# Weights of the last network quantised by VectorE in 36 steps of 512 columns, one in each of 36 rounds of the causal attention

## The reference, cut to what matters

```python
    def lpbq_dequant(w):
        O, I = w.shape
        qmax = 2.0 ** (W_BITS - 1) - 1.0
        wb = w.reshape(O, I // BLOCK, BLOCK)
        s = jnp.maximum(jnp.max(jnp.abs(wb), axis=-1, keepdims=True) / qmax, 1e-12)
        wq = jnp.clip(jnp.round(wb / s), -qmax - 1.0, qmax) * s
        return wq.reshape(O, I)
```

## Time and profile before

| | us |
|---|---|
| median of 3 runs | 1998.86 |
| lowest, highest | 1998.55, 1998.88 |
| profiled execution, its own time | 1991.99 |
| its span | 1990.2 |
| mean granted clock of TensorE, share of full | 0.932 |
| busy: PE, VectorE, ScalarE, GpSimd | 1727.6, 1380.0, 1019.0, 463.2 |

### The profile page before, as it was taken

The page is one execution under the profiler, slowest core; times in us unless marked ns, Lnnn a source line. Parts: engine busy times, 40 slices in busy tenths (PEclk is TensorE's granted clock), DMA queues, the critical chain, the costliest instruction groups (busy, mean ns, idle before and its releaser), DMA issues.

```text
span 1990.2 us, 34704 instructions
## 1 busy us (share of the span) xinstructions
PE 1727.6 (87%) x12889; PEld 1256.4 (63%) x12889; DVE 1380.0 (69%) x4830; ACT 1019.0 (51%) x2647; POOL 463.2 (23%) x501
## 2 busy tenths in 40 slices
PE   3688888888869888999999999999779999979808
PEld 1456666667653455766767766766669989864307
DVE  6877888888335885777776577777566666753785
ACT  5555655555438543555554355555244555533752
POOL 4000000000000223333333234334323333220003
PEclk7798888998979979999999999999889999999859
DMA  5100000000000201000000000000324243300001
GB/s 163 43 1 1 1 1 1 1 1 2 1 1 0 43 21 70 1 1 1 1 2 1 1 1 2 1 1 2 98 64 96 66 96 78 83 1 0 0 0 43
DMA packets 86078, 49.56 MB, mean 25 GB/s; under 512 B 40223, under 2 KB 83669, under 8 KB 85717
## 3 DMA queue, kind: packets, MB, share of 16 engines
q1 hardware_dynamic: 80195, 47.18, 9.1%
q10 hardware_dynamic: 5714, 0.16, 0.2%
HBM read 45.24 MB, written 2.10 MB: 24 GB/s over the span
## 4 chain that ended last, share of the span: by engine, by line
PE 58%; DVE 26%; ACT 9%; issue 4%; POOL 3%; DMA 0%; POOLq 0%; ACTq 0%; DVEq 0%
PE PS L2079 6%; PE PS L1747 6%; DVE nx L774 5%; DVE sq L783 5%; PE PS L1759 5%; PE PS L1772 4%; PE PS L2513 3%; ACT px L1817 3%; PE PS L1733 3%; PE PS L2143 3%; PE PS L1709 3%; PE PS L1787 2%; PE PS L1720 2%; PE PS L2099 2%; PE PS L828 2%
## 5 line engine op out<-in xcount | busy, mean ns | idle before, releaser
L1817 ACT ACTIVATE px<-PS,cnm 128x896 f32<-128x896 f32 (+7 forms) x256 | 189.2, 756 | 285.6 <-DVE cnm L1882 285.6
L1924 POOL TENSOR_SCALAR px<-px,crl 128x640 f32<-128x640 f32 (+7 forms) x128 | 232.3, 1824 | 371.5 <-DVE crl L1893 371.5
L783 DVE TENSOR_SCALAR sq<-nx 128x4 f32<-128x4 f32 x1024 | 175.5, 171 | 31.4
L774 DVE TENSOR_TENSOR_SCAN nx<-sq 128x6 f32<-128x6 f32 x1024 | 174.0, 170 | 32.0 <-POOL sq L913 0.9
L1880 DVE TENSOR_REDUCE cm<-PS 128x1 f32<-128x512 f32 (+3 forms) x224 | 153.9, 687 | 44.6 <-PE PS L1747 44.6
L1759 PE MATMUL PS<-ident,px 128*128 128x128 f32 x1152 | 156.3, 281 | 9.3 <-ACT pT L1830 6.4
L2183 ACT ACTIVATE YT<-YT,xnm 128x154 f32<-128x154 f32 x256 | 104.8, 413 | 92.8 <-DVE xnm L2214 92.8
L198 POOL TENSOR_SCALAR rstd<-mv 128x1 f32<-128x1 f32 x80 | 34.0, 425 | 506.6 <-DVE mv L176 506.5
L1747 PE MATMUL PS<-kT,qT 64*128 64x512 f32 (+3 forms) x768 | 147.9, 503 | 0.4
L1759 PEld LDWEIGHTS PS<-ident,px 128*128 128x128 f32 x1152 | 124.3, 141 | 36.6 <-ACT pT L1830 23.9
L1772 PEld LDWEIGHTS PS<-pT,V 128*64 128x64 f32 x2304 | 124.7, 137 | 34.4 <-issue 32.5
(11 more groups left out here) (336 smaller groups left out, 3855.0 us busy)
## 6 DMA issues: line engine op xcount, KB each, us to landing
xbs<-in_fside_Bx16xSxS SPq DMA_DIRECT2D x8, 1232.0 KB, 6.6
fsrc<-in_fside_Bx16xSxS SPq DMA_DIRECT2D x8, 1232.0 KB, 6.7
xmk<-in_mask_Bx16xSxS_bk SPq DMA_DIRECT2D x8, 308.0 KB, 8.3
fsrc<-in_mask_Bx16xSxS_bk SPq DMA_DIRECT2D x8, 308.0 KB, 8.3
X<-in_x SPq DMA_DIRECT2D x4, 512.0 KB, 6.8
w<-in_L_attn_W_ffn SPq DMA_DIRECT2D x2, 1024.0 KB, 13.0
t<-in_L_ffn_w SPq DMA_DIRECT2D x2, 1024.0 KB, 11.0
out<-xs SPq DMA_DIRECT2D x16, 128.0 KB, 1.7
```

What stands on the lines that cost most here:

```text
L774: e.tensor_tensor_scan(k.nx[:, t % 2, :], d0, d1, 0.0, ALU.mult, ALU.add).then_inc(sem("rec.scan"), 1)
L783: e.tensor_scalar(place(c % 2 * 2 * W6 + 6 * n + 7), state, 10.0, -10.0, ALU.min, ALU.max).then_inc(sem("rec.clip"), 1)
L1817: e.activation(k.px[n % 2][:, h, c0:c1], row[:, c0:c1], ACT.Exp, scale=-1.0, bias=k.cnm[:, h, slot:slot + 1], accum_out=k.cl[:, h, slot:sl ...
L1924: e.tensor_scalar(x, x, k.crl[:, 0, slot:slot + 1], None, ALU.mult).then_inc(sem("c.normal0"), 1)
```

## The change

The twelve `f.weight` steps leave `extra` in `tail_order`. Each matrix is cut into three parts of 512 columns, and each part keeps its four steps: 36 steps `("f.weight", n, part, i)`. Each is appended to `beside` of one round, so it stands at the end of that round for VectorE: after the projections' copies, before the maxima of the next round. The rounds are 10 to 35 (26 steps, in order) and 45 to 54 (10 steps). The maxima and scales of a part fit in 16 columns, `k.fam` and `k.fs`, which are now reused from part to part. The pieces that PE turns wait for the count 21, 42 or 63 of one semaphore, seven operations for each part. The tail keeps 11 `flip` steps and one more, 12 in ten rounds.

```diff
+    weights = [("f.weight", n, part, i) for n in range(3) for part in range(3) for i in range(4)]
+    for n, step in zip([*range(10, ahead - 1), *range(ahead + 8, len(rounds))], weights):
+        beside[n].append(step)
...
     for n, nm in enumerate(k.fraw):
-        extra += [[("f.weight", n, i)] for i in range(4)]
         n0 = len(k.flips)
...
-    def weight(n, i):
-        v = list(k.fraw.values())[n].rearrange("p (b q) -> p b q", q=32)
-        over = lambda t: bass.AP(t, n * bl, [[3 * bl, P], [1, bl], [0, 32]])
+    def weight(n, part, i):
+
+        v = list(k.fraw.values())[n][:, part * 512:(part + 1) * 512].rearrange("p (b q) -> p b q", q=32)
+        over = lambda t: bass.AP(t, 0, [[16, P], [1, 16], [0, 32]])
+        first = 7 * (3 * n + part)
         if i == 0:
             w.wait_ge("load.swiglu", 48)
...
+            w.wait_ge("fw", first)
+            e.tensor_reduce(k.fam[:, :], v, AX.X, ALU.max, apply_absolute_value=True).then_inc(sem("fw"), 1)
+            w.wait_ge("fw", first + 1)
+            e.tensor_scalar(k.fs[:, :], k.fam[:, :], 1.0 / 7.0, 1e-12, ALU.mult, ALU.max).then_inc(sem("fw"), 1)
+            w.wait_ge("fw", first + 2)
+            e.reciprocal(k.fam[:, :], k.fs[:, :]).then_inc(sem("fw"), 1)
         elif i == 1:
...
             e.tensor_tensor(v, v, over(k.fam), ALU.mult).then_inc(sem("fw"), 1)
         elif i == 2:
...
             e.tensor_scalar(v, v, MAGIC, MAGIC, ALU.add, ALU.subtract).then_inc(sem("fw"), 1)
...
             e.tensor_scalar(v, v, 7.0, -8.0, ALU.min, ALU.max).then_inc(sem("fw"), 1)
         else:
-            w.wait_ge("fw", 6 * n + 6)
-            e.tensor_tensor(v, v, over(k.fs), ALU.mult).then_inc(sem("fw.done"), 1)
+            w.wait_ge("fw", first + 6)
+            e.tensor_tensor(v, v, over(k.fs), ALU.mult).then_inc(sem("fw"), 1)
```

More of the change, by code:

```diff
@@ L330, in flip @@
         if kind in ("gate", "up", "down"):
-            w.wait_ge("fw.done", 1 + ("gate", "up", "down").index(kind))
+            w.wait_ge("fw", 21 * (1 + ("gate", "up", "down").index(kind)))
         if ("flip", n) in k.room:
@@ L1530, in causal_tiles @@
     k.crl = sb("crl", [P, 2, 4], scope=inner)
+    k.fam = sb("fam", [P, 16], scope=inner)
+    k.fs = sb("fs", [P, 16], scope=inner)
     k.wqkv = [sb(f"w{n}T", [P, DC, H * 64], scope=inner) for n in "qkv"]
@@ L1952, in cross_tiles @@
 def cross_tiles(k, sb, sc):
-    k.fam = sb("fam", [P, 3, IC * D // 32], scope=sc)
-    k.fs = sb("fs", [P, 3, IC * D // 32], scope=sc)
     k.x1w = {n: sb("x1" + n, [P, DC, H * 64], scope=sc) for n in "qg"}
@@ L2388, in swiglu_vector @@
     sem, at, PS = k.sem, k.order.at, k.PS
-    bl = IC * D // 32
     s = lambda n: k.stp[:, n:n + 1]
-    def weight(n, i):
-        v = list(k.fraw.values())[n].rearrange("p (b q) -> p b q", q=32)
-        over = lambda t: bass.AP(t, n * bl, [[3 * bl, P], [1, bl], [0, 32]])
+    def weight(n, part, i):
+        v = list(k.fraw.values())[n][:, part * 512:(part + 1) * 512].rearrange("p (b q) -> p b q", q=32)
+        over = lambda t: bass.AP(t, 0, [[16, P], [1, 16], [0, 32]])
+        first = 7 * (3 * n + part)
         if i == 0:
             w.wait_ge("load.swiglu", 48)
[L2397 to L2401, removed]
+            w.wait_ge("fw", first)
[4 more added lines that the diff above has]
+            e.reciprocal(k.fam[:, :], k.fs[:, :]).then_inc(sem("fw"), 1)
         elif i == 1:
-            w.wait_ge("fw", 6 * n + 3)
+            w.wait_ge("fw", first + 3)
             e.tensor_tensor(v, v, over(k.fam), ALU.mult).then_inc(sem("fw"), 1)
         elif i == 2:
-            w.wait_ge("fw", 6 * n + 4)
+            w.wait_ge("fw", first + 4)
             e.tensor_scalar(v, v, MAGIC, MAGIC, ALU.add, ALU.subtract).then_inc(sem("fw"), 1)
-            w.wait_ge("fw", 6 * n + 5)
+            w.wait_ge("fw", first + 5)
             e.tensor_scalar(v, v, 7.0, -8.0, ALU.min, ALU.max).then_inc(sem("fw"), 1)
         else:
-            w.wait_ge("fw", 6 * n + 6)
-            e.tensor_tensor(v, v, over(k.fs), ALU.mult).then_inc(sem("fw.done"), 1)
+            w.wait_ge("fw", first + 6)
+            e.tensor_tensor(v, v, over(k.fs), ALU.mult).then_inc(sem("fw"), 1)
     def tile(T):
```

## The result

| | before | after |
|---|---|---|
| median of 4 runs, us | 1998.7 | 1986.36 |
| lowest, highest | 1997.61, 1998.88 | 1985.86, 1988.23 |
| profiled execution, its own time | 1991.99 | 1985.86 |
| its span | 1990.2 | 1984.0 |

After to before is 0.9938, with an interval from 0.9923 to 0.9953. The change gains 12.3 us by the medians, where I had forecast 5.0, and the time lies 0.14 us under my range.

What follows compares the result with a forecast made beforehand. PE was taken to bound the causal attention, VectorE and GpSimd to set the old tail's end. The tail's -17.0 and the causal attention's +12 sum to -5.0 us: 1998.86 becomes 1993.9 us, range 1986.5 to 1999.0.

Steps and rivals of the forecast that it cites:

- What bounds each stage: PE bounds the causal attention, VectorE and GpSimd the old tail; a round's end has 6.6 us of room in nine rounds.
- The tail, -17.0: Tail: without the twelve weight steps its stalls go and PE bounds it, a gain of 17.0 us.
- The walk's end: Tail: PE's work added step by step, the cross attention's first projection starting at 1442.6 to 1443.0 instead of 1459.96.
- The causal rounds, +12: Causal attention: 36 added steps make PE late by 9.3 us, then 2.5 more, 11.8 in all, taken as 12.
- The wait for GpSimd: Causal attention: steps behind VectorE's scaling wait for GpSimd, 0.4 to 0.7 us in four rounds of nine, 1.7 a block.
- The slack of PE, 0.75: Causal attention: late exponentials delay PE only beyond a slack, 0.75 us in five rounds of nine and more elsewhere.
- The price of a step: Causal attention: maximum with scaling and reciprocal 1.20 us, product 0.72, two roundings 0.92; mean 0.89, 8.0 in nine rounds.
- Rival B: Causal attention: steps mostly hide, without GpSimd's wait or with longer PE slack; cost 5.7, net -11.3, 1987.6 us; chance 0.20.
- Rival C: Causal attention: no slack for PE, or dearer steps; cost 15 to 16, net -1.5, 1997.4 us; chance 0.20.
- D: Causal attention: PE stalls in most rounds and its granted clock falls, so the kernel is slower, 2004 us; chance 0.07.
- The edit does not touch what separates them: Whole kernel: the median's 6.9 us above the profiled run was taken to stay, so the forecast starts from 1998.86.
- my own sign for checking: Start of the cross attention: its first projection was to come 5 us earlier if the forecast was right.

Runs made afterwards that it cites:

- early place: The changed kernel with its 36 steps ahead of 1/sum of head 0 instead of at the round's end; rounds 10 to 70 took 539.61 us, ratio 0.9914.
- maxima only: The changed kernel with its products and roundings replaced by maxima over as many columns, weights unquantised; rounds 10 to 70 took 545.54 us, ratio 0.9933.
- five rounds tested: The changed kernel without its 36 steps, one 512-column maximum ending rounds 14, 23, 32, 50 and 59; rounds 10 to 70 took 542.58 us.
- middle place: The changed kernel with each step between VectorE's copy of a turned piece and 1/sum of head 1; rounds 10 to 70 took 543.75 us.

## Why the prediction was right in sign and wrong in size

- **What bounds each stage: right.** PE in the causal rounds, VectorE and GpSimd in the old tail; the idle time ahead of the maxima is the room for a step at a round's end, and that ahead of 1/sum is closed to it. The early place shows that this second room is open to a step put ahead of it.
- **The tail, -17.0: right, 17.9 measured.** The projections follow each other as walked: the last ends 31.7 us after the first starts (31.8 forecast). The walk's end, 1442.6 to 1443.0, is 36.5 to 36.9 us in all, and 36.0 were measured. Of the missing 0.9, 0.4 is that I took the later of the two; most of the rest is that the end was quicker than the 2.6+2.1 us of the walk: the last projection ends at about 1449.3 and the cross attention starts at 1453.61, 4.3 later. No stall is over 2 us, as I had expected.
- **The causal rounds, +12: wrong, 6.3 measured.** The term of the sum that failed is this one, and in it three parts, two of one sign and one of the other. Nine rounds that took 75.5 us took 76.9 (rounds 45 to 53), where I had forecast 78 to 79; rounds 10 to 18, with a step in each, went from 77.2 to 79.3.
  - *The wait for GpSimd, 0.4 to 0.7 us in four rounds of nine (11.8 with it, 5.7 without).* It did not come for the products, and the second of two roundings was at most 0.08 us longer (0.50 for 0.43). The step that failed is the reading of the earlier trace rows: VectorE's scaling ends while GpSimd's pair of operations still runs, hence the product must wait. The line's durations after are 672 to 683 ns for all nine products:

```profile
L2408 DVE TENSOR_TENSOR fsrc<-fsrc,fam x9: 672/676/683, 872.6 to 1254.9; 128x512 f32<-128x512 f32 x9
```

  The nine products of the last step (L2416) took 672 to 682. In round 46 the product starts at 1204.98 (timeline above), 0.07 before VectorE's scaling ends, and GpSimd's pair runs around it:

```profile
1202.40 3.96 POOL L1928 TENSOR_SCALAR px<-px,crl 128x768 f32<-128x768 f32 x2 [6.13 <-DVE crl L1897]
```

  It took 3.43 before, so GpSimd bore the 0.53. VectorE's scaling ends about where GpSimd's first operation does, as I had seen myself; so the product comes where GpSimd's first ends and its second begins (at 1204.89 in this round), and it is the second that gets longer. That it cost 0.3 us at most is what maxima only showed.
  - *The slack of PE, 0.75.* It is nought in the five rounds tested (0.62 us of cost for 0.67 of work). I looked for what PE's next scores need (the exponentials) and took the slack of that one wait; I did not follow ScalarE's queue, where the copies of the turned pieces stand behind the exponential. PE already waited for these before, 3.4 us in the stage, and a wait that is already there has no slack.
  - *The price of a step.* Taken from start to the next instruction's start, kind 0 is 901.20-900.12 = 1.08 us, a product about 0.6 and a pair of roundings 0.8; I had 1.20, 0.72 and 0.92. An instruction that does not need the result of the one ahead starts some 0.08 us before that one ends in the rows, and I had added gaps where the starts overlap. Over 36 steps this is some 4 us of work too much (an estimate from these prices).
  - The direction of each correction is shown: no wait and cheaper steps lower the 12, no slack raises it. How much of the 5.7 us each accounts for, no run separates.
- **Rival B named the cheaper mechanism rightly, and its price by luck.** It said 5.7 without GpSimd's wait and 1987.6. Its 5.7 rests on the slack that is not there and on steps that are too dear, and since 6.3 were measured the two errors nearly cancel. I gave it 0.20. The evidence for it was there: the earlier trace rows show two operations of GpSimd under one row of 3.43 us, and a row for a pair says nothing of what happens between the two.
- **Rival C held half:** no slack for PE, as it said, but not dearer steps. D did not come true: PE lost 6 us in 546, and the granted clock after is 1.00 from 850 to 1270 us.
- **"The edit does not touch what separates them": right, and it spoiled my own sign for checking.** I expected the cross attention's first projection 5 us earlier; it came 6.35 us earlier (1453.61 against 1459.96) though the stages gained 11.5, since 5.2 us were lost ahead of round 10. A point in the span is no measure across two executions; a distance between two rows is. My range's low end, 1986.5, was B's time of 1987.6 less about one us. By the stages alone, -11.5 from the 1998.86 that I started from, the time would be 1987.4, inside the range; the last us lies outside both stages, where executions of one kernel differ by more (856.67 and 860.47 above). So the 0.14 us below the range say nothing of the mechanism; what was wrong is the term of 12. The bounds were narrow even so: the tail's 17.9 lies above its upper bound of 17.5, which I took from the same walk as its value.

## What to carry to other kernels

Filler work belongs ahead of an engine's wait inside the round, not at the round's end: the same 36 steps cost 6.3 us at the end, 4.3 in the middle and 0.1 ahead of the first 1/sum, and two a round cost 14.8 or 0.4. At a round's end the choice of the rounds alone brought 6.3 down to 1.2. To price a delay, follow every queue that the late instruction heads (here ScalarE's copies behind the exponential), and look for a wait of the bounding engine that is already above zero, since through that one a delay is paid in full. Compare stages by the distance between rows that both kernels have, and not by spans or positions, when the clock of untouched stages differs.

## What the runs showed of the hardware

**GpSimd holds VectorE near the start and near the end of a long operation, not in between.** The starts and ends of GpSimd's operations are rough in a profile, but the distances below repeat from round to round to 0.02 us. In the middle place the product starts while a GpSimd scaling has run for 0.41 us. Timelines of GpSimd and of VectorE, and the durations of the line:

```profile
1219.99 2.84 POOL L1931 TENSOR_SCALAR px<-px,crl 128x1024 f32<-128x1024 f32 x1 [3.49 <-DVE crl L1900]
```

```profile
1220.40 1.25 DVE L2411 TENSOR_TENSOR fsrc<-fsrc,fam 128x512 f32<-128x512 f32 x1
```

```profile
L2411 DVE TENSOR_TENSOR fsrc<-fsrc,fam x9: 819/1031/1246, 874.5 to 1254.8; 128x512 f32<-128x512 f32 x9
```

The product takes 1.25 us instead of 0.68, so it waited 0.57 and was through at 1221.65, while GpSimd's operation ended at 1222.83 and was no longer than before. With GpSimd's width of 512, 640, 768, 896 and 1024 columns the product took 0.82, 0.93, 1.03, 1.14 and 1.25 us: the wait grows with the width, but it ends 0.55 to 0.98 us after GpSimd's start, in operations of 1.56 to 2.84 us. Its end does not depend on when the product comes: in one round the product started 0.73 us behind a GpSimd scaling of 1024 columns and took 0.92, so this wait too ended 0.98 after GpSimd's start. A rounding in the same place, which has one input, waited as long: 0.55 to 0.98 us instead of 0.41.

The end of the operation holds VectorE too. Its own scaling of 1024 columns beside GpSimd's of 1024, in before and then in the early place:

```profile
1208.28 1.45 DVE L1899 TENSOR_SCALAR px<-px,crl 128x1024 f32<-128x1024 f32 x1
```

```profile
1206.34 2.84 POOL L1924 TENSOR_SCALAR px<-px,crl 128x1024 f32<-128x1024 f32 x1 [3.15 <-DVE crl L1893]
```

```profile
1214.99 0.75 DVE L1906 TENSOR_SCALAR px<-px,crl 128x1024 f32<-128x1024 f32 x1
```

```profile
1213.55 3.08 POOL L1931 TENSOR_SCALAR px<-px,crl 128x1024 f32<-128x1024 f32 x1 [3.66 <-DVE crl L1900]
```

It starts 1.94 us behind GpSimd's and takes 1.45 us, ending 0.55 after it; started 1.44 behind, it takes 0.75 and is through 0.89 before GpSimd's end. So a wait of 0.7 us comes from the last part of GpSimd's operation, while in between VectorE is not held, and GpSimd's operation is 0.24 longer in this round. Whether a product is held near the end as well no run shows: the ones that came late started 0.2 us or less before an end, and ran in 0.67 to 0.69. The Trainium skill (SBUF — State Buffer, Who interferes with whom) has the port between the two held for a whole instruction; these rows do not agree, and they decide. Its rule that a `tensor_reduce` never contends is borne out: beside a running scaling of GpSimd a maximum took 0.68 us, alone 0.67.

**At a boundary between two of GpSimd's operations VectorE's product goes first,** and GpSimd's next one pays. Its scalings of 256 and of 128 columns in the stage, before and then after:

```profile
L1924 POOL TENSOR_SCALAR px<-px,crl 128x256 f32<-128x256 f32 x14 | 13.2, 945 | 0.0
L1924 POOL TENSOR_SCALAR px<-px,crl 128x128 f32<-128x128 f32 x13 | 8.0, 613 | 0.0
```

```profile
L1928 POOL TENSOR_SCALAR px<-px,crl 128x256 f32<-128x256 f32 x14 | 16.0, 1143 | 0.0
L1928 POOL TENSOR_SCALAR px<-px,crl 128x128 f32<-128x128 f32 x13 | 10.8, 833 | 0.0
```

Means of 0.95 and 0.61 us become 1.14 and 0.83. One of 256 columns that meets a product is 0.52 us longer (0.95 to 1.47, in four of fourteen); one that meets a pair of roundings is 0.33 us longer (1.28), and there the second rounding takes 0.50 instead of 0.43.
